# Attention and routed experts on one core: the expert phase one batch later, the preparation of token groups over eight slots each

## The reference

```
xn = layernorm(x)
q, k, v from xn (k and v through a latent of 64), 16 heads of 64, rotary embedding on q and k
s  = softmax(causal(q k^T / 8)) v, heads joined, times wo
e* = the larger index of the two best of 8 experts (xn @ gate_w + gate_b)
y  = gelu(xn @ w1[e*] + b1[e*]) @ w2[e*] + b2[e*]
out = x + s * silu(2 y)
```

## Time and profile before

| | us |
|---|---|
| median of 3 runs | 316.83 (316.19 to 316.86) |
| time of the profiled execution | 316.45 |
| span in its profile (first to last instruction) | 314.5 |
| PE busy | 290.3 (92% of the span) |
| ACT busy | 241.3 (77%) |
| DVE busy | 223.3 (71%) |
| POOL busy | 217.6 (69%) |

### The profile page before, as it was taken

One profiled execution on the slowest core, in us unless ns is written; L12 is line 12 of the kernel. 1 busy time (PEld: TensorE's weight loads), 2 busy tenths in 40 slices (PEclk: granted clock), 3 DMA queues, 4 the chain that ended last, 5 costly groups with the idle time before them and its releaser, 6 DMA issues.

```text
span 314.5 us, 8401 instructions
## 1 busy us (share of the span) xinstructions
PE 290.3 (92%) x2341; PEld 235.1 (75%) x2341; DVE 223.3 (71%) x883; ACT 241.3 (77%) x845; POOL 217.6 (69%) x321
## 2 busy tenths in 40 slices
PE   1877879999999999999999989999999999999994
PEld 0765668787888888777778779999976777776763
DVE  4878798997868698988898522222258789898651
ACT  3227859787888778989899775555699999899982
POOL 3566967778677787999999953333129998889730
PEclk9999999999999999999999999999999999999998
DMA  7537599953333333334433480000054334344300
GB/s 206 191 89 181 124 295 255 315 162 70 68 71 69 68 70 75 87 97 108 119 91 92 110 218 2 2 0 2 3 149 104 83 92 112 103 107 133 81 17 19
DMA packets 39292, 33.35 MB, mean 106 GB/s; under 512 B 4753, under 2 KB 36370, under 8 KB 39250
## 3 DMA queue, kind: packets, MB, share of 16 engines
q1 hardware_dynamic: 37506, 30.24, 36.9%
q0 software_dynamic: 1024, 2.10, 2.7%
q10 hardware_dynamic: 720, 0.50, 0.6%
HBM read 11.07 MB, written 4.98 MB: 51 GB/s over the span
## 4 chain that ended last, share of the span: by engine, by line
PE 60%; POOL 17%; issue 12%; DVE 5%; ACT 2%; DMA 2%; SPq 1%; ACTq 1%; POOLq 0%; DVEq 0%
PE bank L1062 9%; PE bank L1076 7%; PE bank L1050 7%; PE bank L1090 7%; POOL staged L449 6%; PE bank L1262 6%; PE bank L1247 6%; POOL probs L460 6%; PE bank L1078 3%; PE bank L1023 3%; PE bank L1039 3%; PE bank L1052 2%; DVE rot_out L565 2%; POOL xn L476 2%; POOL sorted_x L468 2%
## 5 line engine op out<-in xcount | busy, mean ns | idle before, releaser
L861 ACT ACTIVATE pexp<-masked,negmax 128x128 f32<-128x128 f32 (+1 forms) x256 | 114.0, 452 | 3.3 <-DVE negmax L574 3.3
L449 POOL TENSOR_TENSOR staged<-rot_out 128x512 f32<-128x512 f32 x64 | 81.9, 1281 | 22.5 <-DVE rot_out L565 19.1
L460 POOL TENSOR_SCALAR probs<-pexp,rden 128x256 f32<-128x256 f32 (+1 forms) x186 | 81.2, 452 | 22.1 <-DVE rden L581 18.8
L574 DVE CUSTOM_DVE_ANT_0 masked<-bank,mask 128x128 f32<-128x128 f32 (+1 forms) x256 | 75.9, 352 | 28.3 <-PE bank L1052 28.0
L565 DVE TENSOR_TENSOR rot_out<-bank,rot 128x1024 f32<-128x1024 f32 x64 | 77.7, 1214 | 1.2 <-PE bank L1025 0.5
L883 ACT COPY probsT<-bank 128x384 f32<-128x384 f32 x128 | 55.2, 481 | 24.0 <-PE bank L1062 23.5
L1062 PE MATMUL bank<-ident,probs 128*128 128x128 f32 x384 | 55.3, 276 | 1.9 <-ACT probsT L883 0.9
L861 ACT ACTIVATION_READ_ACCUMULATOR pexp<-masked,negmax 128x1 f32 x256 | 49.7, 194 | 0.0
L1050 PE MATMUL bank<-qk_sb 64*128 64x256 f32 x256 | 45.0, 428 | 3.1 <-DVE negmax L574 1.6
L1062 PEld LDWEIGHTS bank<-ident,probs 128*128 128x128 f32 x384 | 43.1, 140 | 5.9 <-POOL probs L460 2.4
L1090 PE MATMUL bank<-vo_sb,ctxT 128*128 128x128 f32 x256 | 39.4, 278 | 0.7 <-ACT ctxT L890 0.7
(11 more groups left out here) (106 smaller groups left out, 455.8 us busy)
## 6 DMA issues: line engine op xcount, KB each, us to landing
qk_sb<-staged SPq DMA_DIRECT2D x126, 128.0 KB, 2.7
w_sb<-in_w SPq DMA_DIRECT2D x1, 2048.0 KB, 8.7
w_sb<-in_w SPq DMA_DIRECT2D x4, 512.0 KB, 6.3
sorted_x<-z SPq DMA_DIRECT2D x1, 1408.0 KB, 9.3
sorted_g<-z SPq DMA_DIRECT2D x1, 1152.0 KB, 5.5
out<-res SPq DMA_DIRECT2D x8, 128.0 KB, 1.8
x_sb<-in_x SPq DMA_DIRECT2D x3, 256.0 KB, 3.3
rot<-in_c_rot SPq DMA_DIRECT2D x1, 512.0 KB, 6.3
```

The costliest lines, as they stand in the source:

```text
L449: pool.tensor_tensor(staged[:, n % 2, :, m % 2, :], rot_out[:, m % 2, :, 0:S], rot_out[:, m % 2, :, S:2 * S], op=ALU.add).then_inc(staged_ ...
L460: pool.tensor_scalar(probs[:, g % 2, i, c], pexp[:, g % 2, i, c], rden[:, g % 2, i, k:k + 1], 1.0, ALU.mult, ALU.mult).then_inc(probs_read ...
L574: t = dve.tensor_tensor_reduce(masked[:, g % 2, i, c], s_bank[i][:, c], mask[:, c], -1.0, -NEG * 1e8, ALU.add, ALU.min, negmax[:, g % 2, i ...
L861: e = act.activation(pexp[:, g % 2, i, c], masked[:, g % 2, i, c], ACT.Exp, bias=negmax[:, g % 2, i, k:k + 1], scale=-1.0, accum_out=rowsu ...
```

## The change

- `LEAD` is 6 in place of 5: the experts come ahead of slot 48, and batch 5 goes by `y_keep`.
- Each of the three late token groups has eight slots in place of four: `turn_rows` in slots 3, 11, 19, `latents` in 4, 12, 20, `turn_latents` in 6, 14, 22, `normalise` in 2, 10, 18, `rstd` in 1, 9, 17; the `best` and `best_at` of the last group stand together in slot 24.
- `TWO_J`, `COUNT_SLOT`, `SCATTER_SLOT` and `FIRST_DOUBLE` move eight slots back: 28, 26, 30 and 32.
- The 16 gathers are in slots 51 to 63: two in each of slots 51, 52 and 53, one in each after them.
- Final steps at slots 53, 55, 57, 59, 60, 61 and 63, and in `finish`; each waits also for the final step before it.

```diff
--- before.py
+++ after.py
@@ -38,19 +38,19 @@
 DW = LAT + E
 
 
-LEAD = 5
+LEAD = 6
 G_LEAD = LEAD * NP
 TURNS = ((0, 2), (2, 4), (4, 8), (8, 12), (12, 16))
 W_PARTS = NG
-TWO_J = 20
-COUNT_SLOT = 18
-SCATTER_SLOT = 22
+TWO_J = 28
+COUNT_SLOT = 26
+SCATTER_SLOT = 30
 GATHER_SLOT = G_LEAD + 3
-GATHER_ORDER = (10, 11, 0, 1, 2, 3, 12, 13, 4, 5, 6, 7, 8, 9, 14, 15)
-FINALS = {48: 0, 51: 5, 53: 1, 54: 2, 56: 3, 59: 6, 61: 4}
+GATHERS = ((0, 1), (2, 3), (12, 13), (4,), (5,), (6,), (7,), (8,), (9,), (10,), (11,), (14,), (15,))
+FINALS = {53: 0, 55: 1, 57: 2, 59: 6, 60: 3, 61: 4, 63: 5}
 FINAL_ORDER = tuple(FINALS.values()) + (7,)
 Z_PART = 18
-FIRST_DOUBLE = 3 * NP
+FIRST_DOUBLE = 4 * NP
 ALONE = tuple(range(FIRST_DOUBLE)) + (G_LEAD - 2, G_LEAD - 1, B * NP - 2, B * NP - 1)
 
 
@@ -283,7 +283,7 @@
 
         def scaler(g, i, k):
 
-            busy = SCATTER_SLOT <= g - 1 < SCATTER_SLOT + NT or GATHER_SLOT <= g - 1 < GATHER_SLOT + NT
+            busy = SCATTER_SLOT <= g - 1 < SCATTER_SLOT + NT or GATHER_SLOT <= g - 1
             if g >= B * NP - 3:
                 return ("vector", "pool")[i]
             return "pool" if k or not busy else ("vector", "scalar")[i]
@@ -514,10 +514,11 @@
                     rotated(g + NI)
                 if SCATTER_SLOT <= g < SCATTER_SLOT + NT:
                     scatter(g - SCATTER_SLOT)
-                if GATHER_SLOT <= g < GATHER_SLOT + NT:
-                    gather(GATHER_ORDER[g - GATHER_SLOT])
-                if g in (1, 5, 9):
-                    rstd(2 + g // 4)
+                if GATHER_SLOT <= g:
+                    for n in GATHERS[g - GATHER_SLOT]:
+                        gather(n)
+                if g in (1, 9, 17):
+                    rstd(2 + g // 8)
 
             def experts():
                 ids = [None] * 2
@@ -739,6 +740,7 @@
             def finalise(b):
                 k = FINAL_ORDER.index(b)
                 dve.wait_ge(g_in[b], 32)
+                wait(dve, res_ready, k)
                 g2 = gate[:, 2 * b:2 * b + 2, :].rearrange("p n c -> p (n c)")
                 if b >= LEAD:
                     dve.wait_ge(y_step, NP * b + NP)
@@ -756,48 +758,28 @@
                     take_y(g // NP - 1)
                 if g in FINALS and FINALS[g] >= LEAD:
                     finalise(FINALS[g])
-                if g in (4, 8, 12):
-                    turned_low(g // 4 + 1)
-                if g in (5, 9, 13):
-                    latents_low(g // 4 + 1)
-                if g in (7, 11, 15):
-                    logits(g // 4)
+                if g in (4, 12, 20):
+                    turned_low(g // 8 + 2)
+                if g in (5, 13, 21):
+                    latents_low(g // 8 + 2)
+                if g in (7, 15, 23):
+                    logits(g // 8 + 1)
                 if g + 2 < B * NP:
                     row_max(g + 2)
                 if g + 1 < B * NP and g != G_LEAD:
                     denominators(g + 1)
                     scale(g + 1)
-                if g == 0:
-                    stats(2, 0, 2)
-                if g == 1:
-                    stats(2, 2, 4)
-                    variances(2)
-                if g == 2:
-                    normalise(2)
-                if g == 3:
-                    best(0)
-                    best_at(0)
-                if g == 4:
-                    stats(3, 0, 2)
-                if g == 5:
-                    stats(3, 2, 4)
-                    variances(3)
-                if g == 6:
-                    normalise(3)
-                if g == 7:
-                    best(1)
-                    stats(4, 0, 2)
-                if g == 8:
-                    best_at(1)
-                if g == 9:
-                    stats(4, 2, 4)
-                    variances(4)
-                if g == 10:
-                    normalise(4)
-                if g in (12, 15):
-                    best(g // 4 - 1 if g == 12 else 3)
-                if g in (13, 16):
-                    best_at(2 if g == 13 else 3)
+                if g in (0, 8, 16):
+                    stats(2 + g // 8, 0, 2)
+                if g in (1, 9, 17):
+                    stats(2 + g // 8, 2, 4)
+                    variances(2 + g // 8)
+                if g in (2, 10, 18):
+                    normalise(2 + g // 8)
+                if g in (3, 12, 20, 24):
+                    best((3, 12, 20, 24).index(g))
+                if g in (3, 13, 21, 24):
+                    best_at((3, 13, 21, 24).index(g))
                 if g == 14:
                     dve.wait_ge(c_in, 16 * NC_IN)
                     dve.tensor_copy(cbef16[:], cbef).then_inc(hot_ready, 1)
@@ -958,12 +940,12 @@
                     act.copy(vo_sb[:, 4 * i:4 * i + 4, :].rearrange("p n c -> p (n c)"), bank[2 + i][:]).then_inc(vo_ready, 1)
 
             def slot(g):
-                if g in (4, 8, 12):
-                    turned(g // 4 + 1)
-                if g in (5, 9, 13):
-                    latents_high(g // 4 + 1)
-                if g in (7, 11, 15):
-                    latents_copied(g // 4)
+                if g in (4, 12, 20):
+                    turned(g // 8 + 2)
+                if g in (5, 13, 21):
+                    latents_high(g // 8 + 2)
+                if g in (7, 15, 23):
+                    latents_copied(g // 8 + 1)
                 if g == COUNT_SLOT + 1:
                     act.wait_ge(cnt_done, 1)
                     act.copy(counts[:], w_bank[:, 0:(NT + 1) * E]).then_inc(cnt_read, 1)
@@ -983,8 +965,8 @@
                 turned_probs(g)
                 if more:
                     scale(g + 1)
-                if g in (5, 9, 13):
-                    logits_out(g // 4 + 1)
+                if g in (5, 13, 21):
+                    logits_out(g // 8 + 2)
 
             def finish(b):
                 g = NP * b + NP
@@ -1192,12 +1174,12 @@
                     project(g + NI)
                 if g < B * NP - 2:
                     turn(g)
-                if g in (3, 7, 11):
-                    turn_rows(g // 4 + 2)
-                if g in (4, 8, 12):
-                    latents(g // 4 + 1)
-                if g in (6, 10, 14):
-                    turn_latents(g // 4)
+                if g in (3, 11, 19):
+                    turn_rows(g // 8 + 2)
+                if g in (4, 12, 20):
+                    latents(g // 8 + 2)
+                if g in (6, 14, 22):
+                    turn_latents(g // 8 + 1)
                 if g == COUNT_SLOT:
                     count_tokens()
                 if g > 2 and g - 3 not in ALONE and g not in (G_LEAD, G_LEAD + 1, G_LEAD + 2):
```

## The result

The changed kernel takes 321.47 us (median of 4 runs, 321.06 to 322.65) and the kernel before 316.85 in the same comparison: a ratio of 1.015, with a 95% interval of 1.012 to 1.019. The profiled execution took 321.17 us with a span of 319.2, so 4.7 us more than the 314.5 of before.

What follows compares the result with a forecast made beforehand. PE was taken as the bound, busy 92% of the span. The terms 1.6 + 0.65 + 1.35 - 0.3 = +3.3 us on the profiled 316.45 us gave 319.75, predicted as 319.8 us, range 316.6 to 321.8.

Steps and rivals of the forecast that it cites:

- rival 4: Gathers get longer beside DVE's scaling and final steps, making POOL 1.8 us later: 321.5 us; chance 12%.
- What bounds it: Whole kernel: PE is the bound, busy 92% of the span; other engines cost time only where PE waits for them.
- Preparation, +1.6 us: Slots 10 and 18: PE waits 1.5 us each for `rot_out`; slots that turn rows have no wait; +1.6 us.
- Rival 3: Only the preparation's waits are hidden, for example because `rstd` comes earlier on POOL: 316.7 us; chance 9%.
- Single slots, +0.65 us: Slots 24 to 31 do one pair at a time instead of two, 7.09 us against 6.93: +0.65 us.
- The ground given for the bank: One projection bank through slot 27 costs nothing, as PE is busy in all of 7.09 us with one bank.
- Behind the experts, +1.35 us: Waits in slots 51 and 56 go, some 3 us for POOL over slots 54 to 56 come; net +1.35 us.
- one more is 1.05 us of work and a gap of 0.04: Slots 51, 52 and 53: POOL's cost of one more gather in each, 1.09 us.
- Rival 2: Only POOL's doubled gathers are hidden, POOL starting slot 51 further ahead: 316.7 us; chance 10%.
- Final steps in a busy stretch: Slots 53 and 55: final steps might be 1.7 us longer beside POOL, the sum up to that higher; left out.
- The end, -0.3 us: Slot 60: DVE and ACT take two scaling parts, -0.3 us (bounds 0 and -0.6); last gathers hidden by a little.
- Rival 1: PE's queued work in slot 11 and slots 54 to 56 covers other engines' lateness, all waits go: 313.7 us; chance 7%.

Runs made afterwards that it cites:

- Experiment 2: The changed kernel with the preparation of the token groups every four slots again, as before the change; ratio 1.009 to the kernel before.
- experiment 3: The changed kernel with POOL's `rstd` ahead of its `rotated` in slots 1, 9 and 17; ratio 1.007 to the kernel before, median 319.21 us.
- experiment 6: The changed kernel with double slots from slot 24 on again (`FIRST_DOUBLE` of 3 * NP); ratio 1.021 to the kernel before.
- Experiment 5: The changed kernel with the two gathers of slots 51 to 53 apart, the first ahead of `rotated`, the second behind it; ratio 1.009 to the kernel before.
- experiment 4: The changed kernel with one gather in each of slots 51 to 55, second gathers in 56, 58, 60, 61, and final steps moved; ratio 1.009 to the kernel before.
- experiment 7: The kernel before with only the change's late half (experts ahead of slot 48, its gathers and final steps); ratio 1.008 to the kernel before.

## Why the prediction was right

The mechanism came true in every place that was named, and the sum was too small: +3.3 us forecast, +4.7 measured, of which 0.3 lie ahead of slot 3. That the time is still inside the range is in part luck: its upper end had room for rival 4 and for waits of 2.1 us, and what used that room was mostly neither.

- **What bounds it.** Right: apart from the single slots (PE busy 0.9 us more in all) the loss is waits. No other engine became the bound of more than a few slots.
- **Preparation, +1.6 us.** Right in place and kind, measured +1.8: two waits of 1.43 and 1.44 us (1.5 predicted), no wait in the slots that turn rows. The 0.2 us more are small pieces: slots 9 and 17 take 3.77 us each, where a slot without preparation takes 3.67. Slot 9 takes 3.77 us in the kernel before too. The forecast took this 0.1 us out with the old 0.7 us per group and put back the waits alone. Experiment 2 gives the same 1.8 us from the other side. Rival 3 falls: `rstd` did not come earlier by itself. It has to be put earlier, and experiment 3 shows what that gives.
- **Single slots, +0.65 us.** The +0.6 of the table is worked out from the same two lengths. The changed kernel's trace has both again: 7.09 us in slots 28 and 29 (141.17 to 148.26), 6.93 in slots 40 and 41 (182.44 to 189.37). The ground given for the bank ("costs nothing in slots that have PE busy with one bank") holds for single slots only; experiment 6 shows it false for double ones.
- **Behind the experts, +1.35 us.** Right in place and mechanism (3.0 us of waits in slots 54 to 56, some 3 were forecast), too small in the net. From slot 48 to the point in slot 56 the changed kernel takes 30.16 us (290.94 - 260.78), the old one 55.64 for eight slots more: 30.16 - (55.64 - 27.72) = +2.24. The start was right: the first gather comes 14.08 us behind the beginning of slot 48, as it did behind that of slot 40. The step that failed is "one more is 1.05 us of work and a gap of 0.04". From the end of the first gather to the scaling a second one takes 1.30 us (0.95, and gaps of 0.30 ahead of it and 0.05 behind); the term had no gap ahead of it at all, though the earlier trace rows shows 0.17 even ahead of a gather behind another instruction. Three times 0.21 us are 0.6 of the missing 0.9 us; the other 0.3 us are mostly single gathers longer than the median (1.28 and 1.18 us). Experiment 5 shows that the gap belongs to two gathers in a row. Rival 2 falls: nothing was hidden. Rival 4 said that gathers would get longer; they did, but by 0.1 and 0.2 us, and the larger part is the gap, which it did not name.
- **Final steps in a busy stretch.** Left out of the sum, and right so for slots 53 and 55: their instructions took 0.43 and 0.42, 0.41 and 0.43 us, under a gather. It was DVE's scaling that POOL held up, 1.65 us at 282.79 and 1.39 at 287.72 where 0.29 is usual, and POOL was late in any case. In experiment 4, where POOL was not late, a final step was held for 0.8 us and POOL had to wait behind it.
- **The end, -0.3 us.** Right as a sum: from that point in slot 56 the changed kernel takes 28.26 us and the old one 28.56 (measured to the end of the span). But it is a sum of two things, and only one was named. Slot 60 gave nearly all of its bound, 0.58 us (3.54 for 4.12). Slot 58 took 3.79 us where it took 3.55 in the kernel before. Its transposes lasted 1.12 us in place of 0.88, and the parts of POOL's scaling that they need took 0.82 and 0.63 us where 0.47 is usual, the first beside the final step of slot 57. The last gather is hidden.
- **Rival 1**, that PE's queue covers such lateness, falls with each of the five waits shown, two for `rot_out` and three for POOL.

## What to carry to other kernels

Before spreading preparation over more time, look at what runs beside its longest chain: a step on the bound engine may be covering the wait for a chain on two others, and moved away it lets that wait out in full, here 0.9 us more each time. A helper engine with 0.4 us to spare in a slot can't take a second transfer issue in it; put the second where the engine has lost another duty, and count the gap between two issues. And an instruction that others wait for belongs ahead of one that nobody waits for soon: moving `rstd` by one place took 0.8% off the kernel before.

## What the runs showed of the hardware that was not expected

**The clock after a wait.** In two profiles (experiments 6 and 7) the granted clock fell soon after PE's long wait in slot 54. The time by stretch of experiment 7, slot 50, then 51 to 53, then 54:

```profile
264.83:270.83 6.00, 5.86 (x26) 2.81 (x27) 3.38 (x14) 4.74 (x19) 5.20 (x9) 0.72 0.49 115
270.83:280.63 9.80, 9.80 (x80) 7.99 (x79) 8.21 (x33) 8.67 (x33) 7.70 (x9) 1.00 0.28 74
280.63:288.32 7.69, 6.05 (x33) 3.48 (x31) 5.20 (x15) 4.07 (x16) 6.84 (x10) 0.78 0.40 112
```

The clock was low in slot 50 too. It comes behind a slot in which PE was busy for 2.65 of 3.63 us, and behind a wait of 0.92 us; the changed kernel has 2.65 of 3.63 us and 0.91 us there and a clock of 1.00, and its slot 50 takes 4.41 us. The mean clock in slot 54 is 0.78, that is, part of it at the lower level of 1.2 GHz, and PE is busy 6.05 us with what took it 4.41 in the changed kernel (its slot 54, clock 1.00, with a wait of 1.66 us just as long). The slot is 1.6 us longer by that, but the kernel is not. In slots 55 and 56, where PE waited for POOL in the changed kernel (0.27 and 1.09 us), it now finds POOL ready or nearly so: slots 54 to 56 take 13.77 us here, 13.69 in experiment 6 and 13.70 in the changed kernel. What is left at the end of the span is 0.8 and 0.7 us. The fall in slot 50, where nothing else was late, costs its 1.6 us in full. All this comes in some executions and not in others. What decides it was not tried. The changed kernel's slowest run, 322.65 us, had a mean clock of 0.982; its three others had 0.988 to 1.00.

**POOL holds DVE up for whole instructions.** Besides the final step of the earlier trace rows, POOL's `staged` or scaling held a DVE scaling for 1.65 us, a final step for 1.19 and four normalises for 3.03 (usual: 0.29, 0.42 and 1.7). A held instruction can lose more than one of POOL's: the one of 1.65 us stood through the end of a scaling and all of a `staged`. The gathers did none of this: the instructions of final steps that lay wholly under a gather took 0.41 to 0.43 us. The Trainium skill, page "SBUF — State Buffer", section "Who interferes with whom", gives both cases: a VectorE instruction with two SBUF inputs excludes a GpSimd one that reads SBUF, and a `tensor_scalar` can enter a mode in which it shares a port pair with GpSimd that only one of them holds for a whole instruction. The traces agree.

**Two gathers in a row** leave a gap of 0.30 to 0.31 us between them, in all four pairs of the changed kernel (the pair of slots 62 and 63 is one) and all four of experiment 4; the other runs with such pairs have the same. Behind POOL's `rotated` or scaling a gather started after 0.14 to 0.17 us in all twelve profiles.
